# Six unread identity matmuls behind each half's row sums in a graph network's relational layers

## What is computed

```python
# relational layer (five of them: three of block 0, two of block 2)
msg = h[src] @ W[etype]                       # W[r] of 128 x 128, r in 0..7
agg = segment_sum(msg, dst, 6250)
h   = relu(agg + h @ loopw + bias)            # block 0: + h_prev
# mean layer (blocks 1 and 3)
agg = segment_sum(x[src] * weight, dst) / clip(degree, 1)
h   = concat([x, agg]) @ W.T + b
# after each block
x   = layernorm(x + h)
```

## Time and profile before

| | us |
|---|---|
| median of 3 runs | 8756.66 |
| lowest, highest | 8755.21, 8759.37 |
| span of the profiled execution, first to last instruction | 8614.6 |
| PE busy | 5272.7 |
| DVE busy | 3946.8 |
| POOL busy | 3886.3 |
| ACT busy | 1585.4 |

### The profile page before, as it was taken

The page is one execution under the profiler, slowest core; times in us unless marked ns, Lnnn a source line. Parts: engine busy times, 40 slices in busy tenths (PEclk is TensorE's granted clock), DMA queues, the critical chain, the costliest instruction groups (busy, mean ns, idle before and its releaser), DMA issues.

```text
span 8614.6 us, 134375 instructions
## 1 busy us (share of the span) xinstructions
PE 5272.7 (61%) x26408; PEld 4402.1 (51%) x26409; DVE 3946.8 (46%) x10763; ACT 1585.4 (18%) x3108; POOL 3886.3 (45%) x4125
## 2 busy tenths in 40 slices
PE   5445445656565655555558996555555555555599
PEld 4444444555555555555555554555444554444455
DVE  3222224544444444444546664444444444444566
ACT  1111101222222222222220002222222222222101
POOL 5566554444545444444441004555555555555300
PEclk7677767777778777777778997666667666666799
DMA  2122212333333333323326872232222222222364
GB/s 78 48 55 55 54 52 74 90 88 90 93 92 91 88 87 88 87 83 85 89 85 228 278 253 73 69 72 70 70 70 70 68 70 66 65 67 66 90 188 152
DMA packets 719154, 804.91 MB, mean 93 GB/s; under 512 B 316147, under 2 KB 607471, under 8 KB 718543
## 3 DMA queue, kind: packets, MB, share of 16 engines
q0 software_dynamic: 131872, 271.19, 13.4%
q10 hardware_dynamic: 481717, 270.72, 10.5%
q1 hardware_dynamic: 105210, 259.53, 9.4%
HBM read 529.44 MB, written 277.57 MB: 94 GB/s over the span
## 4 chain that ended last, share of the span: by engine, by line
PE 36%; another core or an unknown queue 30%; issue 17%; SPq 8%; ACT 4%; ACTq 3%; DVE 1%; DMA 1%; DVEq 0%
PE agg L1001 10%; PE msg L1128 7%; SPq L503 7%; PE sum L1117 6%; PE sum L1032 5%; PE msg L1032 4%; ACT bulk L786 3%; ACTq L790 1%; SPq L499 1%; ACT bulk L816 1%; PE lin L974 1%; PE iota_ps L1156 1%; ACTq L160 0%; ACTq L455 0%
## 5 line engine op out<-in xcount | busy, mean ns | idle before, releaser
L685 POOL DMA_INDIRECT bulk<-h_table,srcT_i x3276 | 3095.7, 945 | 3626.3 <-PE sum L1117 1776.7
L1357 DVE TENSOR_TENSOR acc<-msg,acc 128x16 f32 x4160 | 729.4, 175 | 3588.1 <-remote 1927.6
L1001 PE MATMUL agg<-bulk 128*128 128x196 f32 (+1 forms) x3328 | 868.1, 377 | 1658.7 <-ACT bulk L786 1189.9
L1117 PE MATMUL sum<-bulk 128*128 128x128 f32 x8320 | 1480.7, 339 | 199.5 <-issue 153.2
L1117 PEld LDWEIGHTS sum<-bulk 128*128 128x128 f32 x8320 | 1406.4, 252 | 251.5 <-issue 200.0
L786 ACT ACTIVATE bulk<-agg 128x392 f32<-128x392 f32 (+1 forms) x1664 | 825.7, 496 | 3447.0 <-remote 2219.0
L1001 PEld LDWEIGHTS agg<-bulk 128*128 128x128 f32 (+1 forms) x3328 | 532.2, 184 | 1781.4 <-issue 1753.1
L1128 PE MATMUL msg<-bulk,mix_w 128*128 128x128 f32 x4992 | 901.0, 345 | 608.8 <-ACT bulk L816 521.6
L1128 PEld LDWEIGHTS msg<-bulk,mix_w 128*128 128x128 f32 x4992 | 861.2, 257 | 654.2 <-issue 586.6
L816 ACT ACTIVATE bulk<-sum 128x512 f32<-128x512 f32 x1040 | 617.2, 598 | 2246.0 <-remote 1427.2
L685 POOL DMA_INDIRECT bulk<-in_x_dram,srcT_i x819 | 776.1, 948 | 539.6 <-issue 245.5
(11 more groups left out here) (209 smaller groups left out, 2894.8 us busy)
## 6 DMA issues: line engine op xcount, KB each, us to landing
adjacency_w<-bulk ACTq DMA_DIRECT2D x416, 392.0 KB
bulk<-adjacency_w SPq DMA_DIRECT2D x147, 896.0 KB, 4.6
lent<-h_table SPq DMA_DIRECT2D x6656, 0.5 KB
adjacency_n<-bulk ACTq DMA_DIRECT2D x416, 196.0 KB
bulk<-adjacency_n SPq DMA_DIRECT2D x147, 448.0 KB, 4.0
bulk<-h_table,srcT_i POOLq DMA_INDIRECT x3276
lent<-in_x_dram SPq DMA_DIRECT2D x1664, 0.5 KB
bulk<-adjacency_w SPq DMA_DIRECT2D x49, 448.0 KB, 4.1
```

What stands on the lines that cost most here:

```text
L685: nc.gpsimd.indirect_dma_start(out=rows_in[:, s, :], out_offset=None, in_=rows_of[:, :], in_offset=bass.IndirectOffsetOnAxis(ap=srcT_i[:, ...
L1001: last = nc.tensor.matmul(AGG[:, w * LOWS:(w + 1) * LOWS], row[:, w, :], of[:, w, :], start=True, stop=True)
L1117: last = nc.tensor.matmul(SUM[q % 2][:, t * KEYS:(t + 1) * KEYS], rows_in[:, 4 * q + t, :], onehot[:, 4 * q + t, :], start=True, stop=True)
L1357: nc.vector.tensor_tensor(acc[:, at], MSG[h][:, s * WIN:(s + 1) * WIN], acc[:, at], ALU.add).then_inc(added, 1)
```

## The change

Behind the half's sums, PE now waits first for `added`, then runs six fp32 matmuls of `ident` by `ident` into columns 0 to 127 of the half's own message bank, and only then waits for the two copies. Nothing reads what the six write, since the first `msg` matmul starts the bank anew. No semaphore is raised by them.

```diff
 NATURAL = KEYS + LOWS
+UNREAD = 6
...
                                 if between:
                                     between(h, q % 2)
+                            pe.wait_ge(added, k * RING + HALF * h + HALF)
+                            for _ in range(UNREAD):
+                                nc.tensor.matmul(MSG[h][:, 0:HALF * WIN], ident[:, :], ident[:, :], start=True, stop=True)
                             for q in (2 * h, 2 * h + 1):
                                 pe.wait_ge(evacuated[q], k + 1 + h)
-                            pe.wait_ge(added, k * RING + HALF * h + HALF)
                             for n in range(N_RELS):
```

## The result

| | us | runs |
|---|---|---|
| before, on the same chip | 8757.17 (8755.21 to 8759.37) | 4 |
| changed | 9263.74 (9260.93 to 9266.96) | 4 |

The ratio is 1.0582, 95% interval 1.0567 to 1.0597: slower by 507 us, where 8870 was forecast and 9150 was the upper end. The direction was right, the size was that of rival C.

What follows compares the result with a forecast made beforehand. GpSimd's gathers, with pauses between batches set by PE completions told late, were taken to bound the kernel: 8756.7 - 23 (layer 1) + 0 (layers 2, 3) + 130 (layers 5, 6) = 8864, say 8870 us; range 8540 to 9150.

Steps and rivals of the forecast that it cites:

- rival C: Layers 2, 3, 5 and 6: the long pause becomes the rule, up to 510 us lost, 9270 us; chance 0.12.
- B: Filled layers: longer PE burst keeps the clock up, 520 us gained, 8240 us; chance 0.10, alone or with Rival A.
- as written: Layer 1 sign: first bank's copy starts well before the second's, second still "remote", stretch still near 1286 us.
- Rival A: Layer 1: 12 records behind the sums make completions prompt, 230 us gained, 8660 or 8530 us; chance 0.20.
- 23 were taken off: Layer 1: one in ten second-bank completions turns prompt, each saving 2.2 us over 104 halves, 23 us gained.
- Rival D: Whole kernel: all added work hidden, 8757 us, within 0.2%; chance 0.13.
- I take 0: Layers 2 and 3: the later last `agg` is still told at the same time, so 208 halves lose 0 us.
- 130 us: Layers 5 and 6: later `msg` puts nearly all halves on the long-pause side; loss taken between 76 and 153 us.
- the price of 1.3 us a half: Layers 5 and 6: mean pause 3.5 us with `msg` done within 4.5 us of batch start, 4.8 us when later.
- the rule of records: PE completions: with 12 records behind before PE stops 88% late, 8 or fewer nearly all, 16 to 20 one in four.
- The 142 us beside the span: Whole kernel: profiled span of 8614.6 us lies 142 us under the runs' median, a difference kept as it is.

Runs made afterwards that it cites:

- behind_half: Kernel before plus six unread matmuls in the filled halves only, behind the last `agg`, ahead of the next half's sums: 8620.48 us, ratio 1.0011.
- only_layer1: Changed kernel with its six unread matmuls in layer 1 alone, which fills nothing: 8593.49 us, ratio 0.9988.
- wait_first: Changed kernel without the six matmuls, only the wait for `added` ahead of the waits for the copies: 8591.65 us, ratio 0.9988.
- behind_third: Kernel before plus six unread matmuls in the filled halves only, behind the third `agg`, between the two parts of `msg`: 9043.72 us, ratio 1.0513.
- behind_msg_e: Kernel before plus six unread matmuls in the filled halves only, between the last `msg` matmul and the last `agg`: 9238.75 us on chip 8, ratio 1.0529.
- pool_all_b: Kernel before without SyncE's lent rows; GpSimd gathers the sixteenth tile of every fourth turn too, computing the whole reference: 8011.28 us on chip 1, ratio 0.9328.

## Why the prediction was wrong

*What held.* The pause between gathers is what moves, and PE's ends told late set it. The added work itself was free where it met no such end: 4992 more records cost nothing in `behind_half`, 1248 nothing in `only_layer1`, all 6240 nothing on chip 15. The wait cost nothing (`wait_first`). The clock bought nothing: it rose from 0.78 to 0.81 in layer 2 (chip 1) and the layer got 100 us longer, so B fell. The Trainium skill ("TensorE: Matmul & The Clock Gate", why this matters for your kernels) advises keeping TensorE busy for the full clock, and the trace agrees as to the clock. It was worth nothing here: in `behind_half` the same layer stood at 0.84 and the time did not change. In layer 1 the first bank was told earlier than the second and the second still "remote", as written, and the stretch stayed:

```profile
905.00 1.50 PE L1125 MATMUL msg<-ident 128*128 128x128 f32 x12
...
908.17 0.60 ACT L817 ACTIVATE bulk<-sum 128x512 f32<-128x512 f32 x1 [9.01 <-remote]
910.38 0.60 ACT L817 ACTIVATE bulk<-sum 128x512 f32<-128x512 f32 x1 [1.61 <-remote]
...
911.16 0.94 POOL L686 DMA_INDIRECT bulk<-in_x_dram,srcT_i  x1 [2.66 <-remote]
```

The second bank, with 12 records behind it, ended near 905.2 and was copied 5.2 us later. Rival A fell: layer 1 took 1 us more, where 23 were taken off and A had 230. Rival D, no change at all, fell with the result.

*Layers 2 and 3: the step that failed.* "I take 0" stood on a missing tie between the end of `msg` and the next pause, and on one half whose last `agg` was told at the batch's end anyway. Measured: 100 and 96 us. Two faults lie in it. The missing tie does not show that a shift of all halves is free. Looking at the last `agg` in place of `msg` would not have helped: in before the time at which it ends has no tie with the next pause either (correlation 0.07 over some 190 halves of layers 2 and 3). What the spread of halves does hold is at its early end: where the last `agg` ended within 3.6 us of the first gather, 17 of 28 pauses were under 4 us, and 36 of 161 where it ended later. And the one half shown was the common one (55 of 94 pauses of layer 2 were 6 to 7 us), while 17 of 94 were 2 to 3 us: these short ones were there to be lost. Counting how many pauses were still short would have given (6.6 - 2.8) x 17/94 x 104, about 70 us a layer, without any tie.

*Layers 5 and 6: right mechanism, mis-sized term.* 130 us was put on both, 232 measured. There the late ends were sorted rightly, but the price of 1.3 us a half was the difference between two groups that each held short and long pauses. The short ones are 2.7 us, the long ones 5.2 to 5.5, so a half that turns costs 2.6.

*The third `agg` and the rule of records.* "20 records behind is prompt" took an effect for a cause. When the third `agg` is told late, PE stops after the `msg` group behind it, so that only 8 records follow; when it is told in time, the last `agg` and the sums follow too, and there are 20. In the changed kernel (chip 1) 163 of 199 third `agg`s of layers 2 and 3 have 8 behind them and were late, and 28 have 20. `behind_half` is the clean case: it puts 12 further records behind every last `agg`, and of those with 20 behind, 145 of 146 were late in layers 2 and 3. What goes with lateness instead is the time in the batch. Of all ends of the filled layers of before, up to 1.5 us after the first gather at most 1% were late, from 1.5 to 2.5 us a third, from 3.5 us on nine in ten. The changed kernel moved the median third `agg` of layers 2 and 3 from 2.2 to 2.9 us. But time is not all of it: in layers 5 and 6 the third `agg` ended at 3.3 us before and 3 of 137 were late, and in the changed kernel (chip 1) at 2.7 us and 165 of 180 were. Why, stays open; it is the same gap as that of the last `agg` above.

*Rival C* had the right size, with a chance of 0.12: every pause of the filled layers long, 510 us. In `behind_third` and `behind_msg_e` this is literally so (86 of 94 pauses of layer 2 are 6 to 7 us in the latter). In the changed kernel (chip 1) 6 of 84 stay short, 54 are 5 to 7 us and 20 are 7 to 9: the long ones behind a late third `agg` make up for the few that stay short. The ratios, 1.0513, 1.0529 and 1.0566, are close since all three come near the same ceiling.

*The 142 us beside the span* are not what lies around a span, as the text ahead of the prediction had it; that is 2 us. They were the difference between two chips, and the sum should have been made as a ratio.

## To carry over

Where an engine's ends are told late in some stretch of another engine's work, cost an edit by the waits that it can turn from short to long: count those that are still short now, and price each at the full step. A tie that isn't found in the spread of the kernel before does not show that a shift of every case is free. And before a mechanism of waits is built on, compare the span of the trace with the runs beside it: a different chip can remove the mechanism as a whole.

## What the hardware showed

- **Chips differ in whether PE's ends are told in time.** The same kernel takes 8589 us on chip 1, 8604 on chip 2, 8773 on chip 8, and 6363 on chip 15 and 6371 on chip 11. Gathers last 946 ns on both kinds and start every 1.25 us. In the changed kernel's pages GpSimd's idle time before the gathers of L686 from `h_table` is 4245 us on the one and 1678 us on the other; the pauses that late ends make are simply absent. Chip 8 ran after chips 15 and 11, so it is not the hour alone; what sets a chip's kind is open. Chips 1, 2, 8 and 11 were each seen at one time only, so chip and occasion are not fully told apart.
- **SyncE's single-row DMAs add to it**, 558 us here, while on a chip that tells in time 65 further gathers cost 84 us. So the best kernel depends on the chip: `pool_all_b` gains 6.7% on chip 1, and leaving out the lent rows, with the six in the kernel, cost 1.3% on chip 15.
- **The same amount of PE's work costs nothing or 5% by its place.** 4992 records cost nothing measurable behind the last `agg` and 439 us ahead of it, on the same chip, within one half of some 14 us. How an end comes to be told late is open: it comes with gathers in flight, more often with SyncE's single rows, and not by the time in the batch alone.
